# Gate stage of a gated feed-forward kernel: x's integers made from rows and turned by transposing transfers, and one VectorE step moved ahead of another

## What is computed

```python
def act_qdq(x):                       # one scale for the whole tensor
    scale = max(max(|x|) / 32767, 1e-12)
    return clip(round(x / scale), -32768, 32767) * scale
def lpbq_dequant(w):                  # one scale for 32 weights, 4 bits
    s = max(max(|w| over 32) / 7, 1e-12)
    return clip(round(w / s), -8, 7) * s

x = x + tanh(g_xattn) * attention(layernorm(x), ctx)      # x: 4096 x 512
h = act_qdq(layernorm(x))
up   = act_qdq(h @ lpbq_dequant(w_up).T)                  # 4096 x 1536
gate = act_qdq(h @ lpbq_dequant(w_gate).T)
gate = act_qdq(gate * fixed_qdq_u16(sigmoid(gate)))
out = x + tanh(g_ffn) * (act_qdq(gate * up) @ lpbq_dequant(w_down).T)
```

## Time and profile before

| what | value |
|---|---|
| median of three timed executions | 1414.65 us |
| the profiled execution: its own time / span | 1419.34 / 1417.6 us |
| mean granted TensorE clock in it, share of full speed | 0.963 |
| gate stage, first matmul to last job's transposes | 518.0 to 821.2 us |
| busy in 518 to 821: TensorE, VectorE, ScalarE, GpSimd | 282.8, 192.1, 109.6, 42.7 us |
| up stage and its tail | about 826 to 1240 us |
| down stage | about 1240 us to the end |

### The profile page before, as it was taken

One profiled execution on the slowest core, in us unless ns is written; L12 is line 12 of the kernel. 1 busy time (PEld: TensorE's weight loads), 2 busy tenths in 40 slices (PEclk: granted clock), 3 DMA queues, 4 the chain that ended last, 5 costly groups with the idle time before them and its releaser, 6 DMA issues. The chain is left out here.

```text
span 1417.6 us, 19287 instructions
## 1 busy us (share of the span) xinstructions
PE 1288.8 (91%) x6269; PEld 768.2 (54%) x6269; DVE 1008.7 (71%) x1465; ACT 663.8 (47%) x782; POOL 243.2 (17%) x331
## 2 busy tenths in 40 slices
PE   7899999999999989899998999999993039999998
PEld 6688868878878754444444444444441014444443
DVE  0478779878876656666656669997999994545554
ACT  3434344443443223333333268875677984343431
POOL 1124234324313221110011113210110000000000
PEclk9999999999999999999999999999997569999999
DMA  8013212212203355545553489974457863454543
GB/s 326 1 34 94 83 52 75 96 44 83 95 37 105 119 191 181 166 168 192 170 178 119 159 298 351 322 282 146 140 195 299 314 245 126 164 180 155 183 158 116
DMA packets 111244, 228.28 MB, mean 161 GB/s; under 512 B 23121, under 2 KB 35409, under 8 KB 111185
## 3 DMA queue, kind: packets, MB, share of 16 engines
q1 hardware_dynamic: 110896, 227.58, 46.8%
q10 hardware_dynamic: 288, 0.00, 0.0%
HBM read 136.32 MB, written 91.23 MB: 161 GB/s over the span
## 5 line engine op out<-in xcount | busy, mean ns | idle before, releaser
L1278 PE MATMUL gpG<-xph,Wh 128*128 128x512 f16 x384 | 149.3, 389 | 1.1 <-DVE xpl L1189 1.0
L1278 PE MATMUL gpG<-xpl,Wh 128*128 128x512 f16 x384 | 149.2, 388 | 0.0
L1278 PE MATMUL gpG<-xph,Wl 128*128 128x512 f16 x384 | 148.7, 387 | 0.0
L1801 PE MATMUL pD<-Wh,xph 128*128 128x512 f16 x384 | 145.5, 379 | 1.0 <-DVE xpl L1776 1.0
L1278 PE MATMUL pU<-xph,Wh 128*128 128x512 f16 x384 | 145.5, 379 | 0.0
L1278 PE MATMUL pU<-xpl,Wh 128*128 128x512 f16 x384 | 145.5, 379 | 0.0
L1278 PE MATMUL pU<-xph,Wl 128*128 128x512 f16 x384 | 145.5, 379 | 0.0
L1801 PE MATMUL pD<-Wl,xph 128*128 128x512 f16 x384 | 145.5, 379 | 0.0
L1801 PE MATMUL pD<-Wh,xpl 128*128 128x512 f16 x384 | 145.5, 379 | 0.0
L1171 ACT ACTIVATE gst<-gpG,rw 128x512 f32<-128x512 f32 x96 | 66.2, 689 | 161.8 <-PE gpG L1278 161.8
L1202 DVE TENSOR_REDUCE gmx<-gst 128x512 f32 (+1 forms) x96 | 65.6, 684 | 97.9 <-ACT gst L1171 97.7
(11 more groups left out here) (222 smaller groups left out, 2639.5 us busy)
## 6 DMA issues: line engine op xcount, KB each, us to landing
dub<-up_d SPq DMA_DIRECT2D x42, 768.0 KB, 4.8
gate_d<-gst SPq DMA_DIRECT2D x96, 256.0 KB, 2.0
gb<-gate_d SPq DMA_DIRECT2D x24, 768.0 KB, 6.5
up_d<-ust SPq DMA_DIRECT2D x72, 256.0 KB, 4.2
eu<-up_d SPq DMA_DIRECT2D x22, 768.0 KB, 6.1
xr<-xn_d SPq DMA_DIRECT2D x9, 1024.0 KB, 6.0
xin<-in_x SPq DMA_DIRECT2D x32, 256.0 KB, 2.8
x_d<-x SPq DMA_DIRECT2D x32, 256.0 KB, 2.0
```

Of the source, the lines that this page charges most:

```text
L1278: mm = pe.matmul(ps[:, :], Ws[:, it, kt * P:(kt + 1) * P], xs[:, kt, :], start=(kt == 0 and Ws is Wh and xs is xh), stop=(kt == KT - 1 and ...
L1801: mm = pe.matmul(pD[4 * t + q][:, :], os_[n][:, cs], Ws[:, it, :], start=(it == 0 and os_ is oh and Ws is Wh), stop=(it == IT - 1 and os_ ...
```

## The change

Two things change, both in the gate stage.

**x's integers.** TensorE's `transposes` are gone, and with them the semaphore `xT_ps` and the helper `turned`. ScalarE makes the integers from the rows: after eviction `it == 1`, `rows` turns `xr` (SBUF, f32) into a new tile `xi` (`gxi`, 128 x 4 x 512 int16) with four activations, once the tile before has left `xi`. After the store of product 3, SP issues four transposing transfers from `xi` to `xq` in SBUF, 128 x 512 int16 (128 KB) each, all on the semaphore `xt_in`. `high` waits for all four and moves from evictions 5 to 8 to evictions 6 to 9; `low` moves from products 6 to 9 to products 7 to 10. The reload of `xr` waits for `rows` in place of the transposes. The first tile's integers are made as before. There are seven such tiles: 28 transfers in place of 112 transposes.

**The order of two VectorE steps.** `job_integer` at `it == 9` now stands ahead of `job_scales`, and `job_scales` moves on to `it == 10`.

```diff
--- before.py
+++ after.py
@@ -1063,7 +1063,8 @@
         x_out = [sem(f"g_x_out{n}", 32) for n in range(2)]
         st_out = [sem(f"g_st_out{n}", 16) for n in range(NS)]
         xq_done, xh_done, g_ps, g_neg = (sem(f"g_{n}") for n in ("xq", "xh", "ps", "neg"))
-        xT_ps = sem("g_xT_ps", KT)
+        xi = sb(ph, "gxi", [P, 4, H], I16)
+        xi_done, apart, xt_in = sem("g_xi"), sem("g_apart"), sem("g_xt_in", 16)
         xl_done = sem("g_xl", KT)
         g_sb, g_pos = sem("g_sb", 4), sem("g_pos", NS)
         red, xq_first, g_scaled = sem("g_red"), sem("g_xq_first"), sem("g_scaled")
@@ -1081,10 +1082,6 @@
             if q < 3:
                 return by_input(wsc[1], i, q)
             return [d.rearrange("p (i h) -> p i h", h=H)[:, 4 * (q - 3):4 * (q - 3) + 4, bass.ds(i * P, P)] for d in wsc[2]]
-
-        def turned(i, T, kt):
-
-            return at(xT_ps, 2 * KT * i, KT * (T - 1) + kt + 1)
 
         def traffic(sp, i, last=False):
             for t in range(2):
@@ -1100,6 +1097,13 @@
                     sp.wait_ge(*at(g_sb, 2 * IT * i, m + 1))
                     dst = gate_d[bass.ds(8 * i + 4 * t + it // 3, 1), :, (it % 3) * 512:(it % 3 + 1) * 512]
                     sp.dma_start(dst.rearrange("a p k -> (a p) k"), stage[n][:, :]).then_inc(st_out[n], 16)
+                    if it == 3 and not (last and t):
+
+                        sp.wait_ge(*at(xl_done, 2 * KT * i, KT * t))
+                        for q in range(4):
+                            sp.wait_ge(*at(xi_done, 8 * i, 4 * t + q + 1))
+                            sp.sem_inc(apart, 1)
+                            sp.dma_start_transpose(xq[(t + 1) % 2][:, :, q * P:(q + 1) * P], xi[:, q, :]).then_inc(xt_in, 16)
                     if last and t == 1 and it in (2, 5, 8):
 
                         c = it // 3
@@ -1109,7 +1113,7 @@
                     if it == 6 and not last:
 
                         src = four_tiles(xn_d, (2 * i + (t + 3)) % FT)
-                        sp.wait_ge(*turned(i, t + 1, KT - 1))
+                        sp.wait_ge(*at(xi_done, 8 * i, 4 * t + 4))
                         sp.dma_start(xr[(t + 1) % 2][:, :, :], src).then_inc(xr_in[(t + 1) % 2], 16)
                     if it in (2, 6, 10) and not (last and 3 * t + it // 4 + AHEAD >= JR):
                         q = 3 * t + it // 4
@@ -1138,22 +1142,28 @@
 
         @block.scalar
         def _(act):
-            def integer(i, T, kt):
-
-                n = T % 2
-                if T:
-                    act.wait_ge(*turned(i, T, kt))
-                    act.wait_ge(*at(xl_done, 2 * KT * i, KT * (T - 2) + kt + 1))
-                act.activation(xq[n][:, kt, :], pX[kt][:, :], ACT.Copy, scale=INV_X).then_inc(xq_done, 1)
+            def integer(kt):
+
+                act.activation(xq[0][:, kt, :], pX[kt][:, :], ACT.Copy, scale=INV_X).then_inc(xq_done, 1)
+
+            def rows(i, T):
+
+                act.wait_ge(*at(xr_in[T % 2], 16 * i, 16 * (T // 2 + 1)))
+                act.wait_ge(*at(xt_in, 128 * i, 64 * (T - 1)))
+                for q in range(4):
+                    act.activation(xi[:, q, :], xr[T % 2][:, q, :], ACT.Copy, scale=INV_X).then_inc(xi_done, 1)
 
             def high(i, T, kt):
-                act.wait_ge(*at(xq_done, 2 * KT * i, KT * T + kt + 1))
+                if isinstance(i, int) and i == 0 and T == 0:
+                    act.wait_ge(xq_done, kt + 1)
+                else:
+                    act.wait_ge(*at(xt_in, 128 * i, 64 * T))
                 act.wait_ge(*at(x_out[T % 2], 32 * i, 32 * (T // 2)))
                 act.activation(xh[T % 2][:, kt, :], xq[T % 2][:, kt, :], ACT.Copy).then_inc(xh_done, 1)
 
             for kt in range(KT):
                 if kt % 2 == 0:
-                    integer(0, 0, kt)
+                    integer(kt)
                 else:
                     act.wait_ge(xq_first, kt // 2 + 1)
                     act.sem_inc(xq_done, 1)
@@ -1169,11 +1179,10 @@
                         act.wait_ge(*at(st_out[n], 32 * IT // NS * i, 16 * (m // NS)))
                         act.wait_ge(*at(g_pos, 2 * IT * i, m - NS + 1))
                         act.activation(stage[n][:, :], pG[m % 3][:, :], ACT.Copy, scale=row_scale[0][:, it:it + 1]).then_inc(g_sb, 1)
-                        if it == 4 and not (last and t):
-                            for kt in range(KT):
-                                integer(i, t + 1, kt)
-                        if it in range(5, 5 + KT) and not (last and t):
-                            high(i, t + 1, it - 5)
+                        if it == 1 and not (last and t):
+                            rows(i, t + 1)
+                        if it in range(6, 6 + KT) and not (last and t):
+                            high(i, t + 1, it - 6)
                         if it in (3, 7, 11):
                             job_hi(act, J, i, 3 * t + it // 4)
 
@@ -1201,15 +1210,15 @@
                         dve.wait_ge(*at(g_sb, 2 * IT * i, m + 1))
                         dve.tensor_reduce(gmx[:, 1, bass.ds(2 * IT * i + m, 1)], stage[m % NS][:, :], X, ALU.min).then_inc(g_neg, 1)
                         dve.tensor_reduce(gmx[:, 0, bass.ds(2 * IT * i + m, 1)], stage[m % NS][:, :], X, ALU.max).then_inc(g_pos, 1)
-                        if it in range(6, 6 + KT) and not (last and t):
-                            low(i, t + 1, it - 6)
+                        if it in range(7, 7 + KT) and not (last and t):
+                            low(i, t + 1, it - 7)
                         q = 3 * t + it // 4
-                        if it == 9 and t == 0:
-                            job_scales(dve, J, i, 3, row_unit[2][:, bass.ds(i, 1)])
-                        if it == 9 and t == 1 and not last:
-                            job_scales(dve, J, i, 6, row_unit[1][:, bass.ds(3 * i + 3, 3)])
                         if it % 4 == 1:
                             job_integer(dve, J, i, q, (10 * i, 5 * t + 5))
+                        if it == 10 and t == 0:
+                            job_scales(dve, J, i, 3, row_unit[2][:, bass.ds(i, 1)])
+                        if it == 10 and t == 1 and not last:
+                            job_scales(dve, J, i, 6, row_unit[1][:, bass.ds(3 * i + 3, 3)])
                         if it % 4 == 3:
                             job_lo(dve, J, i, q)
 
@@ -1233,14 +1242,6 @@
 
         @block.tensor
         def _(pe):
-            def transposes(i, T):
-
-                n = T % 2
-                pe.wait_ge(*at(xr_in[n], 16 * i, 16 * (T // 2 + 1)))
-                for kt in range(KT):
-                    pe.wait_ge(*at(xq_done, 2 * KT * i, KT * (T - 1) + kt + 1))
-                    turn_rows(pe, pX, xr[n], ident, kt).then_inc(xT_ps, 1)
-
             def gates(i, last=False):
                 for t in range(2):
                     for it in range(IT):
@@ -1253,8 +1254,6 @@
                         else:
                             ready = None
                         product(pe, pG[m % 3], Wh, Wl, xh[t], xl[t], it, ready).then_inc(g_ps, 1)
-                        if it == 3 and not (last and t):
-                            transposes(i, t + 1)
                         if it % 4 == 3:
                             job_turn(pe, J, i, 3 * t + it // 4, ident)
 
@@ -1262,7 +1261,6 @@
             with pe.Fori(0, FT // 2 - 1) as i:
                 gates(i)
             gates(FT // 2 - 1, last=True)
-            pe.wait_ge(*at(xq_done, 0, KT * FT))
             keep_warm(pe, pX[0][:, :], ident, 12)
 
     return (st_out, 16 * FT * IT // NS), (J.stored, 32 * JR * ROUNDS // NJ)
```

## The result

| | before | after |
|---|---|---|
| median of the timed executions | 1416.18 us | 1376.41 us (four executions, 1375.83 to 1376.84) |
| ratio to before, with its 95% interval | | 0.9725 (0.9691 to 0.9760) |
| the profiled execution: own time / span | 1419.34 / 1417.6 us | 1376.84 / 1375.1 us |
| gate stage in it, start of the first matmul to start of the last job's last transpose | 518.0 to 821.2 us | 519.0 to 778.8 us |

The kernel is 39.8 us faster (2.8%) by the medians, 42.5 us by the two profiled executions. The stage took 303.2 us and takes 259.8, 43.4 less. Everything is gained there, and nothing is given back: from the stage's end to the program's it is 596.4 us before and 596.3 after. (What comes ahead of the stage took 1.0 us longer in the profiled execution of the change.)

The account below looks back on a forecast made before the run. TensorE was taken to set the gate stage's pace; removing stalls (21.3), slow clock (7.1) and x's transposes (12.2) made -40.6 us, so 1378.7 or 1374.1 by the reference used; forecast 1375 us, range 1366 to 1390.

Parts of the forecast that it names:

- The seven stalls, 21.3 us: Gate stage: TensorE's seven waits for `gjd` all go once VectorE makes the integer before the scales, saving 21.3 us.
- The slow clock behind them, 7.1 us: Gate stage: matmuls slowed by the halved clock after TensorE's waits return to full pace, saving 7.1 us.
- the rebuilt stage: Gate stage before: products, job turns, transposes, stalls and slow matmuls add to 301.5 of the 302.8 us seen.
- The transposes of x, 12.2 us: Gate stage: TensorE loses 16 transposes in each of seven tiles, 1.74 us a tile, saving 12.2 us.
- The sum: Whole kernel: -21.3 - 7.1 - 12.2 = -40.6 us, giving a forecast of 1375 us.
- VectorE's timetable: Next tile's first `gjd` is done 42.4 us after the earlier tile's start, wanted at 42.8: 0.4 us to spare.
- ScalarE's part: Making x's integers from SBUF takes 0.65 us each, 2.6 us a tile, with nothing on the path.
- The transfers, T = 10.2: Time from 11.6 us into a tile to the last transposing transfer's landing: 8.0 for four, plus 2.2 of queueing.
- The queue ahead: SP's earlier 2.25 MB of transfers, moving until about 13.8 us into the tile, add 2.2 us to T.
- the threshold, 13.9: TensorE stalls at product 10 only from T = 13.9 us on, then 1 us per tile for each us.
- The rival that 1309 ns for a block would have made: Sixteen blocks one after another give T = 23.1, about 1446 us; within the slower case of chance 0.06.
- Nothing given back later: Up stage: its elementwise chain moves forward whole, TensorE's 75.5 us wait with it, so the gain stays.

Follow-up runs that it names:

- order_only: The kernel before with only the change's VectorE order (dequantized tile ahead of the scales), TensorE still turning x: 1388.14 us, ratio 0.9792.
- warm_stall: The kernel before with 10 useless matmuls on the identity put ahead of the job's transposes after product 11: 1410.63 us, ratio 0.9955.
- turn_only: The change with the old VectorE order, so x goes by transfers and the scales stand first: 1408.51 us, ratio 0.9934 to the kernel before.
- scales11: The change with VectorE's scales one product later, at product 11: 1379.61 us, ratio 0.9741 to the kernel before.
- late5: The change with the four transposing transfers issued after the store of product 5, not product 3: 1378.57 us, ratio 0.9735 to the kernel before.
- late6: The change with the four transposing transfers issued after the store of product 6, not product 3: 1394.73 us, ratio 0.9836 to the kernel before.
- one_turn: The change with the four transposing transfers of 128 KB made one of 512 KB: 1375.68 us, ratio 0.9723 to the kernel before.
- jobs_best: The change plus job tiles turned by 256 KB transfers, x's transfers made one, the stage's last job earlier: 1366.20 us, ratio 0.9649 to the kernel before.

## Why the prediction was right, point by point

- **The seven stalls, 21.3 us.** Right: they are gone, and `order_only` shows them going by the order alone.
- **The slow clock behind them, 7.1 us.** Right for the profiled execution, and shown twice: with the stalls gone (`order_only`), and with the stalls filled (`warm_stall`, 6.3 us by the medians, 9.2 in the stage with two other terms). The other executions of the kernel before mostly had a higher clock, so probably fewer slow spells, and less to win.
- **A term left out, 1.7 us.** The seven sets of job transposes behind the stalls took 0.47 to 0.91 us and not 0.44 (0.68 is 596.14 - 595.46 in the earlier trace rows), 1.7 more together. That is what the rebuilt stage lacked: its sum of 301.5 has all 24 sets in it, where the 302.8 ends ahead of the last one.
- **The transposes of x, 12.2 us.** Right: 12.6 us in the stage of `turn_only`.
- **The sum.** 40.6 was forecast; the profiled executions differ by 42.5, the stages by 43.4. The 2.8 us more in the stage are the 1.7 just named and the first matmuls of the stage, which were late by 0.6 us in this execution and by 1.7 in that of before; no edit touches those. The forecast stood against a median of 1414.65; with one more execution it is 1416.18, and the change's is 1.4 above the 1375 forecast. That it came so close is in part luck: it took all of the profiled execution's slow spells off a median execution, which by the clocks has fewer, and left out 2.8 us on the other side.
- **VectorE's timetable.** Right: 0.4 us to spare was worked out and 0.37 is there. `scales11` moved it by one product, and the waits came where and as large as the same arithmetic put them.
- **ScalarE's part.** Mis-sized, without effect: reading from SBUF took 0.709 us, more than 0.65 and more than the 0.69 from PSUM.
- **The transfers, T = 10.2.** Nearly right in the total, with both its parts wrong. Four transfers, one after another at 2.0 us each, were to take 8.0; they take 6.6. Each holds SP for 1.19 us where an ordinary issue takes about 0.35, so four hold it for 5.4 us, but landing, 2.4 us, overlaps with the next ones' issue. The queue ahead was to cost 2.2 us through the bytes that it still moves. It does cost time, but by holding back the issue. In the tile that starts at 584.53, where the scales of w_up stand ahead, SP issues x's stores at 593.34 and 593.78, then product 0's store 9.9 us into the tile (near 8 was forecast; wanted at 13.6, so still hidden), and the first transfer 14.0 us into it and not 11.6. SP's issues, and ScalarE's wait for the landing:

```profile
593.34 0.34 SPq L1092 DMA_DIRECT2D xsh_d<-xph  x1
593.78 0.38 SPq L1092 DMA_DIRECT2D xsl_d<-xpl  x1
594.44 2.52 SPq L1099 DMA_DIRECT2D gate_d<-gst  x3
...
598.53 5.40 SPq L1106 DMA_TRANSPOSE gxq<-gxi  x4
...
605.17 0.63 ACT L1162 ACTIVATE xph<-gxq 128x512 f16<-128x512 int16 x1 [1.19 <-DMA gxq<-gxi]
```

  ScalarE goes on 20.6 us into the tile, so T, from 11.6, is 9.0: 2.4 of delay and 6.6 of transfers. In the other tiles it is 6.5 to 9.0. What carried the forecast was the threshold, 13.9, which `late5` and `late6` enclose; any T below it gives the same time.
- **The rival that 1309 ns for a block would have made** ("VectorE: DVE Perf Modes" of the Trainium skill, "The three transpose paths") did not come. Sixteen blocks landed 6.6 us after the first issue, 0.41 us each, so that figure is not the pace of blocks that follow one another. "As fast as ordinary ones" ("Advanced Engine Details and Errata" of the Trainium skill, section "X-Bar Transpose (TRN2)") is nearer, but not true at every size: an ordinary store of 128 KB lands in 1.9 to 2.2 us and a transposing transfer in 2.4; one of 512 KB takes 5.4 us (`one_turn`), where ordinary stores of that size from SBUF take 2.7 to 3.6.
- **Nothing given back later.** Right: TensorE's wait between up and down is 75.5 us in both kernels. Of the change, the page's group of the matmuls that end it:

```profile
L1290 PE MATMUL pD<-ident 128*128 128x512 f16 x28 | 8.1, 454 | 75.5 <-DVE pmx L1712 75.5
```

## What to carry to other kernels

Where an engine sets the pace, write down a timetable of one period from the starts in the trace, and for each helper the moment from which its lateness reaches that engine: a helper's own waits (52 us of ScalarE's in `late5`) say nothing, the distance to that moment says all. The stalls of TensorE, 1.9 to 3.6 us each, cost a good third more than their length through the clock (7.1 us on 20.1 in the profiled execution); count it where the trace shows it, look for it again at a stage's end, and look at the clock of each execution before you subtract two medians. Work that is moved to the transfer queues takes the issuing queue's time, and at a barrier that queue may be the last one in.

## What the runs showed of the hardware

- A transposing transfer from SBUF to SBUF holds SP's queue: 1.19 us for 128 KB, 1.29 us (median of 24, 1.24 to 2.19) for 256 KB, 2.6 us (`jobs_best`) to 3.1 us (`one_turn`) for 512 KB. To landing it takes 2.4, 3.8 and 4.6 to 5.4 us. Both larger sizes are cheaper for the queue per byte than 128 KB; the cheapest here is 256 KB.
- Within the gate stage, idle times of TensorE up to 1.7 us (`late6`, seventeen of them) were followed by full clock. Of the seven with 1.9 to 3.6 us in the kernel before, five were followed by half the clock for 2 to 4 us, and two, of 3.56 and 1.94 us, were not. In `turn_only`, with the same seven idle times, it was again five, but others: the first one, of 2.48 us, was not followed by it and all three of 3.56 us were. What told them apart was not found.
- ScalarE took 0.709 us to read f32 from SBUF and write 16-bit integers, and 0.692 from PSUM: SBUF was no cheaper for it.
